# Sixty-four-wide graph layer on one core: blocks regrouped as one low group and three high ones, edge rounds in two alternating chains, every chunk beyond nine in the loops

## What is computed

```
msg = concat([x[src], edge_attr]) @ W1 + b1          # 50,000 edges, 64+32 features -> 128
agg = segment_sum(msg, dst, 100000)                  # dst is sorted
y   = x + (concat([x, agg]) @ W2 + b2)               # 100,000 nodes, 64 features
out = (y - mean(y)) / sqrt(var(y) + 1e-5)
```

## Time and profile before

| | |
|---|---|
| median of 3 runs | 696.72 us (695.69 to 697.64) |
| the profiled execution | 697.21 us, span 695.4 us |
| PE matmul busy | 556.4 us (80%) |
| VectorE / ScalarE / GpSimd busy | 457.0 / 394.6 / 425.1 us |
| granted TensorE clock, mean | 0.911 of full |
| HBM traffic | 71 MB, 102 GB/s over the span |

### The profile page before, as it was taken

The page is one execution under the profiler, slowest core; times in us unless marked ns, Lnnn a source line. Parts: engine busy times, 40 slices in busy tenths (PEclk is TensorE's granted clock), DMA queues, the critical chain, the costliest instruction groups (busy, mean ns, idle before and its releaser), DMA issues. The chain is left out here.

```text
span 695.4 us, 27785 instructions
## 1 busy us (share of the span) xinstructions
PE 556.4 (80%) x8394; PEld 505.8 (73%) x8395; DVE 457.0 (66%) x1148; ACT 394.6 (57%) x2012; POOL 425.1 (61%) x419
## 2 busy tenths in 40 slices
PE   1367898988799898898799898889888888873764
PEld 1355788888698897888688897878777777763653
DVE  2687567776657776666657776665788878762443
ACT  0002378887678887777668888776554455532101
POOL 5777737777777777777777777777775454000000
PEclk9957599999989999999989999999999999985665
DMA  2112245455355456546355546544433334220002
GB/s 64 34 36 42 65 134 135 121 153 158 91 153 158 118 134 158 129 123 158 91 146 151 134 131 158 129 122 108 113 92 85 83 83 102 79 60 7 1 1 61
DMA packets 168745, 71.33 MB, mean 103 GB/s; under 512 B 61570, under 2 KB 162447, under 8 KB 168720
## 3 DMA queue, kind: packets, MB, share of 16 engines
q1 hardware_dynamic: 104592, 51.74, 25.8%
q0 software_dynamic: 12544, 12.87, 8.4%
q10 hardware_dynamic: 51584, 6.41, 5.9%
HBM read 45.37 MB, written 25.60 MB: 102 GB/s over the span
## 5 line engine op out<-in xcount | busy, mean ns | idle before, releaser
L393 POOL DMA_INDIRECT feat<-in_x,src_idx x392 | 417.9, 1066 | 159.1 <-issue 121.0
L619 ACT ACTIVATE square<-ps_y 128x64 bf16<-128x64 f32 x784 | 162.7, 239 | 99.1 <-PE ps_y L497 97.0
L506 PEld LDWEIGHTS ps_y<-z_window,onehot 128*128 128x128 bf16 x5664 | 188.5, 99 | 40.8 <-DVE z_window L842 15.6
L506 PE MATMUL ps_y<-z_window,onehot 128*128 128x64 bf16 x5664 | 200.2, 195 | 15.3 <-DVE z_window L842 14.8
L847 DVE TENSOR_TENSOR onehot<-node_of_col,dst_in_group 128x2048 bf16<-128x2048 bf16 x98 | 120.1, 1225 | 78.1 <-issue 68.7
L619 ACT ACTIVATION_READ_ACCUMULATOR square<-ps_y 128x1 f32 x784 | 159.5, 224 | 0.0
L497 PE MATMUL ps_y<-wx,x_t 128*128 128x128 f32 x784 | 117.0, 294 | 26.5 <-ACT x_t L611 23.7
L497 PEld LDWEIGHTS ps_y<-wx,x_t 128*128 128x128 f32 x784 | 99.3, 199 | 31.4 <-ACT x_t L611 28.0
L429 PE MATMUL ps_z<-wz,feat_t 97*128 97x64 f32 x784 | 104.7, 292 | 13.4 <-DVE z_rest L748 13.4
L842 DVE COPY z_window<-z 128x384 bf16 x472 | 115.2, 295 | 0.0
L578 ACT ACTIVATE feat_t<-ps_t 97x512 f32<-97x512 f32 x98 | 58.6, 598 | 98.5 <-PE ps_z L429 72.5
(11 more groups left out here) (125 smaller groups left out, 270.2 us busy)
## 6 DMA issues: line engine op xcount, KB each, us to landing
xin<-in_x SPq DMA_DIRECT2D x97, 256.0 KB
out<-yout SPq DMA_DIRECT2D x97, 256.0 KB
feat<-in_x,src_idx POOLq DMA_INDIRECT x392
feat<-in_edge_attr ACTq DMA_DIRECT2D x96, 64.0 KB
z<-in_src SPq DMA_DIRECT2D x1, 192.0 KB
z<-in_dst SPq DMA_DIRECT2D x1, 192.0 KB
xin<-in_x SPq DMA_DIRECT2D x1, 128.0 KB
out<-yout SPq DMA_DIRECT2D x1, 128.0 KB
```

The source lines that it names most:

```text
L393: nc.gpsimd.indirect_dma_start(out=feat[h][:, feat_at(k) + feat_slot(c), 0:C], out_offset=None, in_=x[:, :], in_offset=bass.IndirectOffset ...
L506: mm = nc.tensor.matmul(ps_y[h][:, col:col + C], onehot[h][:, g, s, a, :], z_window[h][:, g, s, part * C:(part + 1) * C], start=False, sto ...
L619: sq = nc.scalar.activation(square[:, q, :], ps_y[h][:, q * C:(q + 1) * C], ACT.Square, accum_out=sumsq[:, h, q:q + 1])
```

## The change

- **Blocks.** A block is now one low group (nodes 0 to 25,087, `LOW`) and three neighbouring groups of the nodes above. Block 0 has low group 97 (nodes 24,832 to 25,087) and the top of the high part, block 97 has low group 0 and the lowest high groups.
- **Rounds.** Chunks keep their natural order. Even rounds go down from chunks 192 to 199 to chunks 0 to 7, odd rounds from chunks 384 to 391 down to 200 to 207 (`chunk_at`). `block_need` is now a number of rounds. For a group with first chunk f below 200 it is 49 - 2(f >> 3); for a group whose far end max(f + 4, last) is 200 (`HIGH_CHUNK`) or more it is also 98 - 2 max(f >> 3, 25).
- **Steps.** The low group takes 3 chunks at once and the others 2 each (`SLOTS` = 9 in place of 8); the second step is gone, and everything beyond goes in the loops.
- **Transfers.** Loads and stores of a block are two each, 64 KB and 192 KB; SyncE's program is written out in full.
- z_rest lies in a PSUM bank in place of SBUF; the index tables are copied as they stand, with no reversal.

```diff
-STEP = 2 * G + 2
+STEP = 2 * G + 1
...
+LOW = BLOCKS * GN
+HIGH = G - 1
+LOW_ROUND = PAIRS // 2
+HIGH_CHUNK = (LOW_ROUND + 1) * 2 * CB
...
+SLOTS = 3 + 2 * HIGH
+TAKEN = (3, 2, 2, 2)
+SLOT = (0, 3, 5, 7)
...
-        z_rest = sb("z_rest", [P, 2 * CB, C])
+        z_rest = ps("z_rest", [P, 2 * CB * C])[:, :].rearrange("p (k c) -> p k c", c=C)
...
+        def chunk_at(k):
+
+            at = k % 2 * (2 * CB * LOW_ROUND + CB) + (2 * CB * LOW_ROUND - CB * k)
...
+            def load_x(k, h):
+                b = 2 * k + h
+                wait_rounds(sp, x_used[h], k)
+                sp.dma_start(xin[h][:, 0, :], low_part(x, b)).then_inc(x_loaded[h], 16)
...
+                    sp.dma_start(xin[h][:, 1:G, :], high_part(x, b)).then_inc(x_loaded[h], 16)
...
-                with pe.If(second > 0):
-                    for g in range(G):
-                        nc.tensor.reg_add(seconds_done, seconds_done, 1)
-                        turn_no = pe.snap(seconds_done)
-                        pe.wait_ge(window2_ready, turn_no)
-                        pe.wait_ge(hot2_ready, turn_no)
-                        pair_sum(g)
...
+                with pe.If(further > 0):
+                    _, firsts = load_steps(mybir.EngineType.PE, b, 0, G, CHUNKS - 4)
+                    _, pairs = load_steps(mybir.EngineType.PE, b, G + 1, G, CHUNKS // 2)
...
-            link(nc.vector.tensor_scalar(need[:, :], first[:, :], 3.0, None, ALU.add))
-            link(nc.vector.tensor_tensor(need[:, :], need[:, :], last[:, :], ALU.max))
+            link(nc.vector.tensor_scalar(last[:, :], last[:, :], -1.0, None, ALU.add))
+            link(nc.vector.scalar_tensor_tensor(out=far_first[:, :], in0=first[:, :], scalar=4.0, in1=last[:, :],
+                                                op0=ALU.add, op1=ALU.max))
+            link(nc.vector.tensor_scalar(first_round_i[:, :], steps[:, 0:G], 3, None, ALU.arith_shift_right))
+            link(nc.vector.tensor_copy(first_round[:, :], first_round_i[:, :]))
+            link(nc.vector.tensor_scalar(need[:, :], first_round[:, :], -2.0, float(2 * LOW_ROUND + 1), ALU.mult, ALU.add))
+            link(nc.vector.scalar_tensor_tensor(out=need[:, :], in0=first[:, :], scalar=float(HIGH_CHUNK),
+                                                in1=need[:, :], op0=ALU.is_lt, op1=ALU.mult))
+            link(nc.vector.tensor_scalar(first_round[:, :], first_round[:, :], float(LOW_ROUND + 1), -2.0, ALU.max, ALU.mult))
+            link(nc.vector.tensor_scalar(first_round[:, :], first_round[:, :], float(2 * PAIRS), None, ALU.add))
+            link(nc.vector.scalar_tensor_tensor(out=far_first[:, :], in0=far_first[:, :], scalar=float(HIGH_CHUNK),
+                                                in1=first_round[:, :], op0=ALU.is_ge, op1=ALU.mult))
+            link(nc.vector.tensor_tensor(need[:, :], need[:, :], far_first[:, :], ALU.max))
             link(nc.vector.reduce_max(block_need[:, :], need[:, :], axis=AX.X))
-            link(nc.vector.tensor_scalar(block_need[:, :], block_need[:, :], 1.0, None, ALU.add))
             nc.vector.tensor_scalar(lacking[:, :], round_chunks[:, :], block_need[:, :], blocks_left[:, :],
                                     ALU.is_lt, ALU.mult).then_inc(s_lacking, 1)
```

More of the change, by code:

```diff
@@ L333, in _ @@
[L333 to L342 removed]
+                sp.wait_ge(out_stored[h], 16 * transfers(PAIRS, h))
@@ L410, in _ @@
                 pe.sem_inc(y_done[s])
-            ea_loads = (2, 1)
             def turn(k, h, half=None):
@@ L498, in dense, with slots_sum @@
                                             wx[:, :], start=False, stop=(g == G - 1))
-                def pair_sum(g):
-                    for s in range(2):
+                def slots_sum(g, chunks):
+                    for slot in range(SLOT[g], SLOT[g] + chunks):
                         for a in range(A):
@@ new lines, in block_sum @@
+                        with pe.If(pairs[g] > 0):
+                            with pe.Fori(0, pairs[g]) as n:
+                                nc.tensor.reg_add(pairs_done, pairs_done, 1)
+                                done = pe.snap(pairs_done)
+                                chunk = nc.s_assert_within(
+                                    pe.snap(firsts[g] + 2 * n), 0, CHUNKS - 2 - TAKEN[g],
+                                    skip_runtime_bounds_check_because="the table of steps ends every range before the last chunk")
+                                for s in range(2):
+                                    pe.wait_ge(hotx_ready[s], done)
+                                    for a in range(A):
+                                        col = (g * A + a) * C
+                                        for part in range(3):
+                                            mm = nc.tensor.matmul(ps_y[h][:, col:col + C], onehot_x[s][:, a, :],
+                                                                  z[:, chunk + (TAKEN[g] + s), part, :], start=False, stop=False)
+                                    mm.then_inc(hotx_used[s], 1)
@@ new lines, in one_hots @@
+                        with dve.If(pairs[g] > 0):
+                            with dve.Fori(0, pairs[g]) as n:
+                                nc.vector.reg_add(pairs_done, pairs_done, 1)
+                                turn_no = dve.snap(pairs_done)
+                                chunk = nc.s_assert_within(dve.snap(firsts[g] + 2 * n), 0, CHUNKS - 2 - TAKEN[g], skip_runtime_bounds_check_because="the table of steps ends every range before the last chunk")
+                                for s in range(2):
+                                    dve.wait_ge(hotx_used[s], turn_no)
+                                    nc.vector.tensor_scalar(onehot_x[s][:, :, :], node_of_col[:, :, :], base,
+                                                            dst_of[:, bass.ds(chunk + (TAKEN[g] + s), 1)],
+                                                            ALU.add, ALU.is_equal).then_inc(hotx_ready[s], 1)
```

357 lines of the change are left out of this document (157 added, 200 removed).

## The result

| | before | after |
|---|---|---|
| median | 696.45 us (695.69 to 697.64, 4 runs) | 1007.16 us (1003.79 to 1008.8, 4 runs) |
| ratio of after to before | | 1.4453 (1.4407 to 1.4499) |
| the profiled execution | 697.21 us, span 695.4 | 1005.89 us, span 1004.0 |
| granted TensorE clock, mean | 0.911 | 0.706 |

A forecast was written before the change was run, and what follows sets the result against it. TensorE bound the overlapped stage before; changed, gathers bound an edge stage and units follow. 513 (gathers, hand-over) + 348 (units) + 67 + 27 + 32 (loops, clock) + 7 (end) = 994 us span, so 996 us; range 935 to 1065.

The forecast's parts named there:

- The table: Table `units`: block 0 counts as needing 48 rounds, holds all others back, so no unit runs beside a gather.
- Edge stage: All gathers before any unit, bound by gathers alone at 1.255 us each, ending at 506.2 us; upper end 553.6.
- Hand-over: From last gather to first one-hot: 6.6 us, so the units start at 513.
- Unit pitch: Time per unit once gathers are done: 7.1 us, ends 6.8 and 8.2; 49 units make 348 us.
- Loops, clock, end: Unit stage: 18 loop entries 67 us, 18 further turns 27, low clock 32; after the last dense product 7.
- Rival 1: TensorE's clock stays low in the unit stage, 4.6 us more for 42 further units: 1189 us; chance 0.06.
- Rival 2: SyncE's queue of stores, grants and loads becomes the bound, loads 2 us late a unit: 1094 us; chance 0.04.
- Rival 3: The table is released and units run beside gathers: ends at 689 or 674 us, 1 to 3% faster; chance 0.04.

The follow-up runs named there:

- y1: Changed kernel with first + 2 in place of first + 4 in a group's far end, plus a check of bounds; normal condition: 782.1 us, ratio 1.1173.
- y2: Kernel before with AHEAD = 0, all units after the last round, plus a check of bounds; normal condition: 985.13 us, ratio 1.4082.
- x1: Changed kernel with only the check of bounds on the unit counts added; slow condition: 1134.29 us, ratio 1.0573.
- x4: Kernel before with only the check of bounds on the unit counts added; slow condition: 1077.65 us, ratio 1.006.

## Why the prediction was right, and where a part was not

**The table** was the whole of the forecast, and it was read rightly: 196 + 4 = 200 fires the test, `open_block` is 0, and no one-hot of a unit starts before 527.2. y1 shows that this one number is the cause: with 198 in place of 200 the overlap is back. y2 shows from the other side that a held table costs 287 us with nothing else of the change in the kernel.

**Edge stage.** Forecast end 506.2, measured 509.33 + 0.94 = 510.3. The choice of 1.255 us a gather over 1.376 was right; the measured pitch is 1.266. The reason fits too. A gather took 1.066 us on average beside the units and takes 0.945 here; in y2, the kernel before with nothing beside its gathers:

```profile
L393 POOL DMA_INDIRECT feat<-in_x,src_idx x392 | 378.4, 965 | 131.2 <-issue 123.7
```

GPSIMD Engine Reference, section Key points, of the Trainium skill names VectorE instructions with two SBUF inputs as what GpSimd contends with. These rows agree: with no unit beside them the gathers take 0.10 to 0.12 us less each. The runs take away all of VectorE's work for the units at once, so they do not tell which of its instructions it is.

**Hand-over.** Forecast 6.6 us, measured 527.17 - 510.27 = 16.9. This was the worst term. I let one round's messages follow the last gather and priced them at 1.0 us. In fact two rounds follow each other, and sixteen messages take 3.5 us at low clock, as the earlier trace rows had it.

**Unit pitch.** Forecast 7.1, taken above the 6.96 of the sum in case VectorE or SyncE had a say. Measured 6.93, close to TensorE's sum alone. 49 units: 8 us too many.

**Loops, clock, end.** Forecast 67 + 27 + 32 + 7, measured 129 + 7.5. The first three were measured only together, so that the sum is right says little of each. Within it a turn was a little too cheap: 1.60 us, where I had 1.49.

Together: 994 + 4.1 (gathers) + 10.3 (hand-over) - 8.3 (pitch) + 3 to 4 (loops) + 0.3 = 1004, the measured span. That the forecast came within 1.1% owes something to these signs being different.

**Rival 1** (clock stays low) fell: the clock is 0.89 over the stretch from 530 to 600 us and 1.00 from 600 to 700 and from 700 to 800. **Rival 2** (SyncE) fell: the queue has over a microsecond free in each unit.

**Rival 3** was wrong in its price, though its condition did not occur in the change as given. "It ends at 476 + 15 + 198 = 689": y1 has 781.5. The 476 was the first second step, which lies in the 39th pass of the kernel before (reciprocal at 478.44); the 39th of y1 is at 523.98. Up to there I had at most 15 us and it was 45.5. Of these, 24.7 come by the fourth pass and were not in the sum at all, though the counts of the loops in the same prediction name "5 in blocks 0 and 1". The other 20.9 are the extra matmuls and, beside them, the longer waits for x_t, a part of which may be the check of bounds. From there on I had 11 x 10.5 + 60 + 22 = 198 us, and it was 781.5 - 523.98 = 257.5. The 7 us of the end were left out of the 198. The 10.5 us a unit had no row, and I added no price for the low clock, though the forecast for the held case had one, 4.6 us a unit. Eleven of these are 51, so by my own price 58 of the 59.5 us missing there are named; no run takes the low clock away to test it in the normal condition. So the side that I gave the released kernel, faster than before, was wrong, and by more than its range.

## What to carry to other kernels

A table that releases work in order is only as good as its strictest row. Work out every row by hand from the real data, first of all the rows that stand first in the order, and look at a margin ("+ 4") against the nearest boundary. When overlap is lost, the time is the sum of the stages, each at the pace that it has alone, and the trace of before often has a short stretch in which one of them already runs alone; that stretch is the price list. Work that is moved into a loop with a turn-by-turn wait costs its turns and also the clock of everything around it, so a rival that moves the loops somewhere else must carry the clock too. And a check that goes into every kernel of a series is a change as well: its price has to be taken in the condition in which the deciding kernels run.

## What the runs showed of the hardware that I had not expected

The same program takes 697 us in one set of runs and 1063 to 1076 in another, steadily within each. The kernel before, with the check of bounds, in the slow one. First two entries of its waits (engine and line, waited for, us in all, times, longest):

```profile
POOL feat L393 <- PE ps_t L421: 443.2, 44, 20.1
PEld ps_y L506 <- issue: 318.4, 349, 2.0
```

In the normal condition the first of these was 31.4 us. And TensorE in a block's window matmuls, the first block after the program has come back from a round:

```profile
568.24 0.93 PE L506 MATMUL ps_y<-z_window,onehot 128*128 128x64 bf16 x26
569.52 0.19 PE L506 MATMUL ps_y<-z_window,onehot 128*128 128x64 bf16 x1 [0.34 <-issue]
570.96 0.19 PE L506 MATMUL ps_y<-z_window,onehot 128*128 128x64 bf16 x1 [1.25 <-issue]
572.37 0.19 PE L506 MATMUL ps_y<-z_window,onehot 128*128 128x64 bf16 x1 [1.23 <-issue]
...
577.39 1.08 PE L506 MATMUL ps_y<-z_window,onehot 128*128 128x64 bf16 x16 [1.23 <-issue]
```

After 26 matmuls at full pace come six single ones, up to 1.4 us apart, then the rest at full pace. Nothing that the profile records holds them. The 48 matmuls took 1.56 us in the earlier trace rows and take 10.2 here. Now x1, the held change, in the same condition, in its edge stage and its unit stage:

```profile
66.00:500.00 434.00, 204.97 (x837) 176.32 (x837) 58.52 (x126) 77.29 (x136) 253.65 (x270) 0.52 0.16 31
700.00:800.00 100.00, 94.87 (x1932) 89.22 (x1929) 82.33 (x191) 81.19 (x528) 0.00 (x0) 1.00 0.51 152
```

The edge stage has 837 matmuls where the same stretch had 1052 in the normal condition. The unit stage has 1932 in 100 us where the row of the normal condition has 1939: it is hardly slowed. So the time is lost mainly in the rounds' loop, where each turn jumps over the units or into them, and not in the loop over units. In x1 it does not show as broken rows of matmuls: around 210 us ScalarE stands 15.38 us before a copy to feat_t, with a releaser that the profile does not name, and TensorE waits 11.77 us for the edge attributes that ScalarE loads behind it. Held, the last gather starts at 626.1 us in place of 509.3, 117 us later, of the 137 by which the span of x1 is longer (1140.8 against 1004.0). Released, 1127.44 us against 782.1, pauses in the units' own matmuls would come on top, as in the rows of x4. That fits held and released coming out alike in this condition, but no run parts the two.

Runtime: NRT & Kernel Launch, section Instruction fetch mechanics, of the Trainium skill says that a taken branch to a target outside the window at hand must wait for its instructions to be fetched. The profile counts no fetches. That the time is lost where the rounds' loop jumps fits such a cause; that the pauses of x4 come 26 matmuls into a block, and not at its start, does not speak for it. Why they are there on some occasions and not on others, the chip or where the program lies, no run here tells. It stays open.
